# The preparation stage of an RWKV block: next batch's mixes issued ahead of the keys, the normalising affine and two biases moved off VectorE, loops written out

## The reference

```python
x = layernorm(hidden)                       # no gain, no bias
delta = shifted - x                         # shifted: the token before, zero at the start
xr, xw, xk, xv, xa = (x + delta * x_m for m in "rwkva")
r, k, v = xr @ W_r, xk @ W_k, xv @ W_v
log_w = -softplus(-(tanh(xw @ w_lora_a) @ w_lora_b + w_lora_bias)) - 0.5
a = sigmoid(xa @ a_lora_a @ a_lora_b + a_lora_bias)
g = sigmoid(r @ g_lora_a) @ g_lora_b + g_lora_bias
kk = k * k_k;  kk = kk / max(norm_per_head(kk), 1e-12)
k = k * (1 + (a - 1) * k_a)
o = scan(r, log_w, k, v, -kk, kk * a)       # the next stage
bonus = sum_per_head(r * k * r_k) * v
```

## Time and profile before

| | us |
|---|---|
| median of 3 runs | 4496.63 |
| lowest and highest of them | 4488.98 and 4498.77 |
| the profiled execution | 4498.68 |
| its span in the trace | 4497.0 |
| of it PE busy | 3958.5 |
| DVE busy | 3213.0 |
| ACT busy | 2185.5 |
| POOL busy | 2053.9 |

### The profile page before, as it was taken

One profiled execution on the slowest core, in us unless ns is written; L12 is line 12 of the kernel. 1 busy time (PEld: TensorE's weight loads), 2 busy tenths in 40 slices (PEclk: granted clock), 3 DMA queues, 4 the chain that ended last, 5 costly groups with the idle time before them and its releaser, 6 DMA issues. The chain is left out here.

```text
span 4497.0 us, 72210 instructions
## 1 busy us (share of the span) xinstructions
PE 3958.5 (88%) x23448; PEld 2701.7 (60%) x23448; DVE 3213.0 (71%) x8691; ACT 2185.5 (49%) x7329; POOL 2053.9 (46%) x1670
## 2 busy tenths in 40 slices
PE   5999999999996696888849999999999999846698
PEld 2344444444435464666538888888888888745566
DVE  5777777877746111889869999999999999855310
ACT  2666666666665111544404555556555555503311
POOL 2211221221223321112258888888888888632522
PEclk7999999999996798999979999999999999976699
DMA  4322332332347132244353232323232222186332
GB/s 110 82 75 70 99 80 67 91 83 65 75 96 224 63 130 80 103 168 168 149 101 39 34 42 34 42 34 42 35 41 36 39 37 38 14 283 209 130 126 80
DMA packets 495672, 395.16 MB, mean 88 GB/s; under 512 B 298634, under 2 KB 457637, under 8 KB 489184
## 3 DMA queue, kind: packets, MB, share of 16 engines
q1 hardware_dynamic: 483040, 365.68, 33.0%
q0 software_dynamic: 12288, 25.28, 1.7%
HBM read 230.52 MB, written 167.97 MB: 89 GB/s over the span
## 5 line engine op out<-in xcount | busy, mean ns | idle before, releaser
L749 DVE TENSOR_REDUCE at_neg_max<-at_slot 128x1 f32<-128x512 f32 (+3 forms) x1216 | 746.1, 655 | 247.5 <-PE at_slot L541 244.7
L671 ACT ACTIVATE at_prob<-at_slot 128x512 f32<-128x512 f32 (+1 forms) x1216 | 631.1, 577 | 354.8 <-PE at_slot L561 353.8
L1722 PE MATMUL sc_added<-sc_outer,sc_ident 128*128 128x128 f32 x4096 | 585.9, 286 | 79.3 <-POOL sc_outer L1473 58.2
L1722 PEld LDWEIGHTS sc_added<-sc_outer,sc_ident 128*128 128x128 f32 x4096 | 496.4, 191 | 210.1 <-DVE sc_state L1623 115.4
L1486 POOL TENSOR_TENSOR sc_terms<-sc_seen,sc_pack 128x1024 f32<-128x1024 f32 (+2 forms) x288 | 605.6, 2150 | 13.7 <-PE sc_ps_o L1744 13.7
L1744 PE MATMUL sc_ps_o<-sc_terms,sc_ident 128*128 128x256 f32 x2048 | 607.0, 381 | 2.1 <-POOL sc_terms L1486 2.1
L389 POOL TENSOR_SCALAR_AFFINE_SELECT at_prob<-at_prob 128x512 f32<-128x512 f32 x256 | 162.8, 636 | 888.3 <-ACT at_prob L671 888.1
L1646 ACT ACTIVATE sc_seen<-sc_state 128x512 f32<-128x512 f32 x256 | 152.8, 597 | 757.1 <-DVE sc_decayed L1587 748.1
L541 PE MATMUL at_slot<-at_k_stack,at_q_stack 96*128 96x512 bf16 (+3 forms) x1536 | 459.4, 335 | 22.2 <-DMA at_k_stack<-parts 19.8
L1473 POOL TENSOR_TENSOR sc_outer<-sc_pack 128x2048 f32<-128x2048 f32 x128 | 467.3, 3671 | 5.0
L561 PE MATMUL at_slot<-at_q_stack,at_k_stack 99*128 99x512 bf16 (+3 forms) x1536 | 452.7, 331 | 12.2 <-ACT at_prob L671 11.8
(11 more groups left out here) (251 smaller groups left out, 7164.1 us busy)
## 6 DMA issues: line engine op xcount, KB each, us to landing
packed<-pr_pack SPq DMA_DIRECT2D x16, 3072.0 KB, 13.4
sc_pack<-packed SPq DMA_DIRECT2D x512, 96.0 KB, 3.6
parts<-at_parts SPq DMA_DIRECT2D x96, 256.0 KB
f_up_w<-in_ffn_wi SPq DMA_DIRECT2D x16, 1024.0 KB
f_down_w<-in_ffn_wo SPq DMA_DIRECT2D x16, 1024.0 KB
at_q_stack<-parts SPq DMA_DIRECT2D x32, 384.0 KB
at_k_stack<-parts SPq DMA_DIRECT2D x32, 384.0 KB
slots<-at_no_row SPq DMA_DIRECT2D x2, 4128.0 KB
```

Source lines behind the costliest of these rows:

```text
L671: act.activation(prob[:, first:first + n, q1 - tiles * P:q1], ps[:, 0:n * tiles * P].rearrange("p (n k) -> p n k", n=n), ACT.Exp)\
L749: dve.tensor_reduce(neg_max[:, chunk, qt, h:h + n], ps[:, 0:n * tiles * P].rearrange("p (n k) -> p n k", n=n), AX.X, ALU.max, negate=True) ...
L1722: pe.matmul(added[h][:, 0:HALF], ident[:], outer[m % 2][:, 2 * n + s, h * HALF:(h + 1) * HALF], start=(s == 0), stop=False)
```

## The change

The order of a turn is new. The steps of the next batch are split: `normalise` becomes `stats` (bn_stats, bn_aggr, epsilon), `root` (ACT's square root) and `affine`. The next batch's mixes r and w now stand ahead of this batch's `key`, and its mix a ahead of `bonus`; mix a of a batch was the turn's own work before. `w_inner` goes ahead of `turn_r`, and the product of g ahead of `a_inner`. `turn_x` goes behind `v`.

`affine` writes `xn` on ACT: DVE makes the reciprocal and a new 128x8 `shift` (minus mean by reciprocal), then ACT runs eight activations of the form x * rstd + shift. Before, DVE ran eight tensor_scalar.

The biases of w and a become row 65 of `w_inner_b` and `a_inner_b`, against a row of ones in `w_inner` and `a_inner` that POOL writes once. DVE's bias additions for w and a (L2140) go, and ACT takes the sigmoid straight from PSUM, so that ACT, not DVE, frees those slots. g keeps its addition on DVE.

The hardware loops of the stage become Python loops, so every turn's instructions are written out, with constant waits in place of register values.

```diff
-PREPARE_USER = {"turn_x": "act", "r": "act", "turn_r": "act", "w_inner": "act", "g_inner": "act", "w": "dve",
-                "a_inner": "act", "g": "dve", "a": "dve", "v": "act", "k": "dve"}
+PREPARE_USER = {"turn_x": "act", "r": "act", "turn_r": "act", "w_inner": "act", "g_inner": "act", "w": "act",
+                "a_inner": "act", "g": "dve", "a": "act", "v": "act", "k": "dve"}
...
-    return [("normalise", 0), ("turn_x", 0), ("turn_x", 1), ("mix", "r"), ("mix", "w")]
+    return [("stats", 0), ("root", 0), ("affine", 0), ("turn_x", 0), ("turn_x", 1), ("mix", "r"), ("mix", "w"), ("mix", "a")]
...
-    return (halves("r") + halves("turn_r") + [("w_inner", 0), ("g_inner", 0), ("mix", "a")]
-            + plus([("normalise", 0)]) + halves("w") + [("mix", "v"), ("a_inner", 0)] + halves("g") + halves("a") + [("mix", "k")]
-            + plus(halves("turn_x")) + halves("v") + plus([("mix", "r")]) + halves("k")
-            + halves("key") + plus([("mix", "w")]) + halves("bonus"))
+    return (halves("r") + [("w_inner", 0)] + halves("turn_r") + [("g_inner", 0)] + halves("w") + [("mix", "v")]
+            + plus([("stats", 0)]) + halves("g") + [("a_inner", 0)] + halves("a") + plus([("root", 0), ("affine", 0)])
+            + [("mix", "k")] + halves("v") + plus(halves("turn_x") + [("mix", "r")]) + halves("k") + plus([("mix", "w")])
+            + halves("key") + plus([("mix", "a")]) + halves("bonus"))
...
-        inner_b = {"w": sb("w_inner_b", [RW, C]), "a": sb("a_inner_b", [RW, C]), "g": sb("g_inner_b", [RG, C])}
-        wide = {m: sb("wide_" + m, [P, C]) for m in ("k_k", "k_a", "r_k", "w", "a", "g")}
+        inner_b = {"w": sb("w_inner_b", [RW + 1, C]), "a": sb("a_inner_b", [RW + 1, C]), "g": sb("g_inner_b", [RG, C])}
+        wide = {m: sb("wide_" + m, [P, C]) for m in ("k_k", "k_a", "r_k", "g")}
...
+        shift = sb("shift", [P, TILES])
-        inner = {"w": sb("w_inner", [RW, T]), "a": sb("a_inner", [RW, T]), "g": sb("g_inner", [RG, T])}
+        inner = {"w": sb("w_inner", [RW + 1, T]), "a": sb("a_inner", [RW + 1, T]), "g": sb("g_inner", [RG, T])}
...
-            with eng.Fori(0, BATCH - 1) as b:
+            for b in range(BATCH - 1):
...
-            loads += [(inner_b[m][:], src) for m, src in (("w", w_b), ("a", a_b), ("g", g_b))]
+            loads += [(inner_b["w"][0:RW, :], w_b), (inner_b["a"][0:RW, :], a_b), (inner_b["g"][:], g_b)]
+            loads += [(inner_b["w"][RW:RW + 1, :], spread(w_bias, 1)), (inner_b["a"][RW:RW + 1, :], spread(a_bias, 1))]
             loads += [(wide[m][:], spread(src)) for m, src in
-                      (("k_k", k_k), ("k_a", k_a), ("r_k", r_k), ("w", w_bias), ("a", a_bias), ("g", g_bias))]
+                      (("k_k", k_k), ("k_a", k_a), ("r_k", r_k), ("g", g_bias))]
...
-            with sp.Fori(0, BATCH - 2) as b:
+            for b in range(BATCH - 2):
...
             own.up(pool.memset(turned[:], 0.0))
+            own.done()
+            for m in "wa":
+                own.link(pool.memset(inner[m][RW:RW + 1, :], 1.0))
...
-                    if stage == "normalise":
+                    if stage == "root":
                         act.wait_ge(var_ready, 1 + f + 1)
                         act.activation(std[:], mean_var[:, :, 1], ACT.Sqrt).then_inc(std_ready, 1)
+                    elif stage == "affine":
+                        act.wait_ge(affine_ready, 1 + f + 1)
+                        for n in range(TILES):
+                            act.activation(xn[:, n, :], x[:, n, :], ACT.Identity, bias=shift[:, n:n + 1],
+                                           scale=rstd[:, n:n + 1]).then_inc(xn_ready, 1)
...
-                        act.wait_ge(z_used, 1 + b * 4 + what + 1)
+                        slots.wait_read(act, ("w", what))
...
                     elif stage == "w":
-                        slots.wait_read(act, (stage, what))
-                        act.activation(z["w"][what][:], z["w"][what][:], ACT.Sigmoid).then_inc(z_used, 1)
+                        act.wait_ge(w_packed, 1 + b * 2)
+                        act.activation(z["w"][what][:], ps[:], ACT.Sigmoid).then_inc(emptied[s], 1)
                     elif stage == "a":
-                        slots.wait_read(act, (stage, what))
-                        act.activation(a_sig[what][:], a_sig[what][:], ACT.Sigmoid).then_inc(z_used, 1)
+                        if b:
+                            act.wait_ge(chain, 1 + (b - 1) * TURN + 5 * (what + 1))
+                        act.activation(a_sig[what][:], ps[:], ACT.Sigmoid).then_inc(emptied[s], 1)
...
-                reader = {"r": ("r", 1), "w": ("v", 1), "a": ("r", 1), "v": ("w_inner", 0), "k": ("a_inner", 0)}[m]
+                reader = {"r": ("r", 1), "w": ("v", 1), "a": ("k", 1), "v": ("w_inner", 0), "k": ("a_inner", 0)}[m]
...
-                    if stage == "normalise":
+                    if stage == "stats":
...
+                    elif stage == "affine":
                         dve.wait_ge(std_ready, 1 + f + 1)
+                        dve.wait_ge(xn_ready, 1 + f * TILES)
                         in_start.link(dve.reciprocal(rstd[:], std[:]))
-                        for t in range(TILES):
-                            dve.tensor_scalar(xn[:, t, :], x[:, t, :], mean_var[:, t, 0:1], rstd[:, t:t + 1],
-                                              ALU.subtract, ALU.mult).then_inc(xn_ready, 1)
+                        dve.scalar_tensor_tensor(out=shift[:], in0=rstd[:], scalar=-1.0, in1=mean_var[:, :, 0],
+                                                 op0=ALU.mult, op1=ALU.mult).then_inc(affine_ready, 1)
...
-                    elif stage in ("w", "a"):
-                        slots.wait_filled(dve, s, use)
-
-                        if stage == "w":
-                            dve.wait_ge(w_packed, 1 + b * 2)
-                        else:
-                            dve.wait_ge(z_used, 1 + b * 4)
-                        dve.tensor_tensor(by_tile(z[stage][what][:]), by_tile(slot[s][:]), wide_of[stage], ALU.add)\
-                           .then_inc(emptied[s], 1)
...
-                        dve.wait_ge(z_used, 1 + b * 4 + 2 + what + 1)
+                        slots.wait_read(dve, ("a", what))
```

More of the change, by code:

```diff
@@ L1849, in prepare @@
         std_ready = sem("std_ready")
+        affine_ready = sem("affine_ready")
         xn_ready = sem("xn_ready")
@@ L1855, in prepare @@
         emptied = [sem(f"emptied{s}") for s in range(PREPARE_SLOTS)]
-        z_used = sem("z_used")
         w_packed = sem("w_packed")
@@ L1878, in run @@
             part(Slots(start, [0] * PREPARE_SLOTS, filled, emptied), None, 0)
-            with eng.Fori(0, BATCH - 1) as b:
+            for b in range(BATCH - 1):
                 part(turn_counts(turn, b), b, b + 1)
             part(turn_counts(last_turn, BATCH - 1), BATCH - 1, None)
+        START, TURN = 2 * TILES + 1 + KC, 2 * 6
         def field(h, f):
@@ L1971, in _ @@
         def _(pe):
-            pe.wait_ge(consts, 1 + 3)
+            pe.wait_ge(consts, 1 + 5)
             def wait_mixed(b, m):
@@ L2031, in _ @@
         def _(act):
-            act.wait_ge(consts, 1 + 3)
+            act.wait_ge(consts, 1 + 5)
             def part(slots, b, f):
@@ L2062, in part @@
                         width = inner_a[m].shape[2]
-                        act.activation(inner[m][:], ps[0:width, :],
+                        act.activation(inner[m][0:width, :], ps[0:width, :],
                                        {"w": ACT.Tanh, "a": ACT.Copy, "g": ACT.Sigmoid}[m]).then_inc(emptied[s], 1)
                     elif stage == "w":
-                        slots.wait_read(act, (stage, what))
-                        act.activation(z["w"][what][:], z["w"][what][:], ACT.Sigmoid).then_inc(z_used, 1)
+                        act.wait_ge(w_packed, 1 + b * 2)
+                        act.activation(z["w"][what][:], ps[:], ACT.Sigmoid).then_inc(emptied[s], 1)
                     elif stage == "a":
-                        slots.wait_read(act, (stage, what))
-                        act.activation(a_sig[what][:], a_sig[what][:], ACT.Sigmoid).then_inc(z_used, 1)
+                        if b:
+                            act.wait_ge(chain, 1 + (b - 1) * TURN + 5 * (what + 1))
+                        act.activation(a_sig[what][:], ps[:], ACT.Sigmoid).then_inc(emptied[s], 1)
                     elif stage == "key":
@@ L2080, in _ @@
         def _(dve):
-            dve.wait_ge(consts, 1 + 3)
-            START, TURN = 2 * TILES + 1 + KC, 2 * 6
+            dve.wait_ge(consts, 1 + 5)
             wide_of = {m: wide[m][:].unsqueeze(1).broadcast_to([P, HALF_TILES, C]) for m in wide}
```

## The result

| | before | changed |
|---|---|---|
| median, us | 4495.52 (4 runs, 4488.98 to 4498.77) | 4528.05 (4 runs, 4527.33 to 4530.43) |
| profiled span | 4497.0 | 4525.6 |
| DVE busy | 3213.0 | 3150.0 |
| ACT busy | 2185.5 | 2196.2 |

The ratio is 1.0075, with a 95% interval of 1.0059 to 1.0091: 32.5 us more in the medians and 28.6 in the profiled spans, where the forecast's sum was 44.8 (4541, range 4512 to 4580).

The account below looks back on a forecast made before the run. DVE was taken to set the 57.95 us lap before, and a chain through ACT after: 11.4 + 6 x (63.7 - 57.95) - 1.1 = 44.8 us on the profiled 4498.7, then 2.0 off for the median: 4541 us, range 4512 to 4580.

Parts of the forecast that it names:

- The closed chain through ACT: From one batch's key end to the next's, waits through ACT's in-order list close a circle of 62.2 us, against 57.95 before.
- The walk: Step-by-step timing of one preparation lap in the new order, from second key half's end to the next: 62.2 us.
- TensorE's clock, +1.5 a lap: PE running at 1.2 GHz after idle gaps, on w_inner, adds 0 to 2.4 us a lap; 1.5 taken.
- I take the middle and a bit: Choice of 1.5 us for slow PE clock, giving 63.7 us a lap, with near ends 62.2 and 64.6.
- The first turn, +11.4: Stage start to the first key's second-half end: 95.0 us, the middle of 96.0 and 93.9, against 83.6.
- The last lap, −1.1: The last batch prepares no next batch: 50.7 us plus 1.5 for PE's clock, against 53.3.
- The rest of the program, 0: Stages outside preparation: the change touches only the preparation stage, so no difference was counted there.
- What costs nothing: Bias rows 0 to 0.1 us a product, POOL's fills hidden before x lands, written-out loops saving 0 to 0.3 a turn.
- POOL's contention "no gain, no loss": POOL's product with r_k slows the mix beside it; mix v now pays those 2 us instead of mix a.
- Signs in the trace: Expected in the changed trace: reciprocal waits 6 to 7 us, delta about 9, DVE share about 70%, laps 62 to 65.
- DVE stays the bound: Rival: gaps stay hidden and each preparation lap falls by DVE's saved 7.4 us, total 4447 us; chance 0.11.
- The drain of 1.38 us: Skill page's extra cost behind each ACT table load: an estimated 2.8 us more a lap, sum 4563; not adopted.

Follow-up runs that it names:

- a2_act_extra: The changed kernel with one more unused ScalarE copy in each of seven turns, between a's sigmoids and the root; mean lap 63.17 us, ratio 1.0096 to the kernel before.
- a3_dve_extra: The changed kernel with four more unused VectorE reductions in each of seven turns, ahead of the reciprocal; mean lap 62.33 us, ratio 1.0085 to the kernel before.
- b1_written_out: The kernel before with only the preparation stage's hardware loops written out; mean lap 58.28 us, ratio 1.0011 to the kernel before.
- a7_plan: The changed kernel reordered: w's product and statistics earlier, root before a_inner, affine after its copy, turn_x before v; mean lap 50.15 us, ratio 0.9876 to the kernel before.

## Why the prediction was right, and where it was off

- **The closed chain through ACT: right.** The walk gave 62.2 us, the lap measured by it 61.8, and every step on the way lies within 0.4 us (though this lap has a share of low clock that the walk left out, next point). `a2_act_extra` and `a3_dve_extra` show that time on it counts in full and time beside it not.
- **TensorE's clock, +1.5 a lap: 0.5 too much, on a walk that was 1.0 too long.** The low clock came where it was expected: behind 2.51 idle the first half of r took 5.38 us in five of seven turns (granted 0.68, so at 1.2 GHz for a part), and behind 5.39 `w_inner` took 4.98 to 6.59 (granted 0.70 in the lap shown, 0.55 in the longest). It ended there: `turn_r` ran in 1.97. ACT's row of `r_rows` and tanh's load covered only a part of it. The activation of `w_inner` waited 0.44 to 2.05 us, 0.99 in the mean, and the laps follow `w_inner` one to one. Without low clock they would be 61.2 (an estimate: 56.64 and the 4.54 us up to which `w_inner` is covered). So the walk's 62.2 is close to the mean of 62.16 by luck. Of the 1.0 us too much in it, 0.4 are `r_rows`: it ends at 3.3, not 3.7, in part because the gap of 0.23 ahead of it went with the hardware loop. The mis-sized step is "I take the middle and a bit", 63.7 for 62.16. That difference makes 9.2 of the 16.2 us by which the sum of 44.8 lies over the 28.6 of the spans (the medians differ by 32.5): 6 × (63.7 − 62.16).
- **The first turn, +11.4: 1.5 short.** Of 96.0 and 93.9 the prediction took the middle; r's product ran at the low clock for longer than before, 9.91 us (granted 0.72), and the time came out at 96.5.
- **The last lap, −1.1: measured −3.0.** Of the 1.5 us for the clock 0.5 came (`w_inner` 5.03, its activation waited 0.49), and the walk's 50.7 was again too long.
- **The rest of the program, 0: measured −7.1.** Its code is the same. In the other kernels on such chips that rest was between 3974 and 3983 us, so this is how executions differ, and no effect that the change was shown to have. It hides part of the stage's 35.7 us, so that part of the small total is luck.
- **What costs nothing: right.** The two fills took 0.94 us each and POOL was through at 1767.4, before `x` landed for the statistics at 1769.62. The products with 65 rows take 3.62 to 3.69 us, where 64 took 3.72. The loops' 0 to 0.3 us a turn show in the shortest laps (57.12 in `b1_written_out`, 57.31 before), but not in the kernel's time.

```profile
1764.77 0.94 POOL L1953 MEMSET pr_w_inner<- 1x1024 f32 x1
...
1767.14 0.29 POOL L1955 TENSOR_SCALAR_AFFINE_SELECT pr_ident<-pr_ident 128x128 f32<-128x128 f32 x1 [0.15 <-POOL pr_ident L1954]
1769.62 2.70 DVE L2121 BATCH_NORM_STATS2 pr_stats<-pr_x 128x6 f32<-128x256 f32 x8 [20.70 <-DMA pr_x<-x_mixed]
...
1789.34 9.91 PE L2002 MATMUL pr_slot<-pr_big_r,pr_mixed_r 128*128 128x256 f32 x32 [6.18 <-DVE pr_mixed_r L2107]
```

- **POOL's contention "no gain, no loss": right.** Mix v takes 4.6 for its pair, mix a 2.5.
- **Signs in the trace.** In the lap shown the reciprocal waits 6.78 and `delta` 9.20 (forecast 6 to 7 and about 9); over the seven turns the reciprocal waits 6.27 to 9.82, `delta` 9.20 or 9.21; PE is idle 2.51 before r's first half but only 0.32 before its second (forecast 2.3), since the first half at low clock filled that gap (2.00 in the two turns where that half ran in 3.69); before `w_inner` 5.39 (over 5). DVE's share is 67%, not 70. Three tables are loaded a turn, as forecast, where the kernel before loaded five. Their number says little: `a7_plan` loads five again, and its laps are the shorter ones.
- **The rivals.** "DVE stays the bound" fell: with 7.4 us less on DVE neither order got a shorter lap, until the order was made for the chain. The drain of 1.38 us that the Trainium skill ("ScalarE: Activation LUTs", What ACT_TABLE_LOAD costs) puts behind each table load, by which the sum would have been 4563, doesn't show in this trace: the root follows its load at once (1950.02 + 1.28, then 1951.31).
